# Wkv products from PSUM on VectorE, half-array matmuls in pairs, and a new instruction order in a fused RWKV decoder layer

## The reference

```python
# 1. RWKV layer, on h = layernorm(layernorm(x)); hh is h one token earlier
xk, xv, xr = (h * tm + hh * (1 - tm) for tm in (att_tmk, att_tmv, att_tmr))
k, v, sr = xk @ Wk.T, xv @ Wv.T, sigmoid(xr @ Wr.T)
# wkv, token by token, w = -exp(time_decay), u = time_first:
#   y = (e1*aa + e2*v) / (e1*bb + e2), with qq = max(pp, u + k); then aa, bb, pp move on
x = x + (sr * wkv(w, u, k, v)) @ Wo.T
x = x + sigmoid(xr2 @ Wrec.T) * (square(relu(xk2 @ Wkey.T)) @ Wval.T)
# 2. attention across the 16 heads of one token, causal in the head index, keys and values = ctx
x = x + softmax(mask(q_h . ctx_h / 4)) @ ctx_h
# 3. low-rank FFN of rank 64
x = x + (gelu((x @ U1) @ V1 + b1) @ U2) @ V2 + b2
```

## Time and profile before

| | |
|---|---|
| median of 3 runs | 1357.65 us (1354.46 to 1358.54) |
| the profiled execution's own time | 1354.16 us |
| its span | 1352.4 us |
| instructions | 14723 |
| mean granted TensorE clock | 0.920 |
| DMA | 38.39 MB, 28 GB/s on average |

### The profile page before, as it was taken

The page is one execution under the profiler, slowest core; times in us unless marked ns, Lnnn a source line. Parts: engine busy times, 40 slices in busy tenths (PEclk is TensorE's granted clock), DMA queues, the critical chain, the costliest instruction groups (busy, mean ns, idle before and its releaser), DMA issues.

```text
span 1352.4 us, 14723 instructions
## 1 busy us (share of the span) xinstructions
PE 1090.1 (81%) x3584; PEld 610.2 (45%) x3584; DVE 1076.3 (80%) x2108; ACT 1063.3 (79%) x2134; POOL 982.2 (73%) x847
## 2 busy tenths in 40 slices
PE   0479587979899897979899897979899897959626
PEld 0136354544546363544546363544536363535302
DVE  1454898898989799797989798897989798876681
ACT  8878778888888878888888878888888878566435
POOL 0211896969696988968696978968696978877580
PEclk9889789999999899999999899999999899969667
DMA  5010010001010100101010100101010100110000
GB/s 171 16 38 10 16 32 16 31 17 47 16 47 1 62 0 16 47 16 47 16 47 2 61 0 16 47 16 47 16 47 7 41 1 16 32 32 16 0 16 16
DMA packets 38961, 38.39 MB, mean 28 GB/s; under 512 B 2930, under 2 KB 38644, under 8 KB 38900
## 3 DMA queue, kind: packets, MB, share of 16 engines
q1 hardware_dynamic: 38900, 37.77, 8.7%
HBM read 29.38 MB, written 8.39 MB: 28 GB/s over the span
## 4 chain that ended last, share of the span: by engine, by line
PE 40%; DVE 23%; ACT 18%; POOL 10%; issue 7%; DMA 1%; ACTq 0%; DVEq 0%; POOLq 0%; SPq 0%
PE bank L844 16%; PE bank L920 5%; POOL prod L337 5%; PE bank L926 5%; DVE o_att L1367 5%; PE bank L851 4%; ACT n L470 4%; POOL prod L349 4%; DVE stat L1178 4%; PE bank L912 3%; PE bank L897 2%; PE bank L936 2%; PE bank L930 2%; PE bank L858 1%; DVE num L1289 1%
## 5 line engine op out<-in xcount | busy, mean ns | idle before, releaser
L349 POOL TENSOR_TENSOR prod<-prob,v_dh 128x256 f32<-128x256 f32 (+3 forms) x256 | 404.7, 1617 | 41.4 <-ACT prob L587 23.5
L337 POOL TENSOR_TENSOR prod<-q,kv_ctx 128x256 f32<-128x256 f32 (+5 forms) x448 | 405.6, 944 | 32.9 <-ACT q L470 32.9
L844 PE MATMUL bank<-xk,w_key 128*128 128x512 f32 x512 | 238.4, 614 | 20.2 <-DVE xk L1220 14.2
L1335 DVE TENSOR_REDUCE score<-prod 128x16 f32<-128x256 f32 (+5 forms) x448 | 177.2, 466 | 76.6 <-POOL prod L337 76.6
L897 PE MATMUL bank<-w_val,hidden 128*128 128x256 f32 x1024 | 229.4, 380 | 0.0
L359 POOL TENSOR_TENSOR num<-kT,vT 128x512 f32<-128x512 f32 x32 | 46.6, 1455 | 240.3 <-PE bank L851 181.5
L897 PEld LDWEIGHTS bank<-w_val,hidden 128*128 128x128 f32 x1024 | 193.4, 191 | 31.7 <-issue 7.1
L1367 DVE TENSOR_REDUCE o_att<-prod 128x64 f32<-128x256 f32 (+3 forms) x256 | 189.5, 801 | 10.0 <-POOL prod L349 10.0
L844 PEld LDWEIGHTS bank<-xk,w_key 128*128 128x128 f32 x512 | 98.7, 197 | 142.4 <-issue 117.3
L858 PE MATMUL bank<-ident,n 128*128 128x128 f32 x384 | 63.2, 311 | 123.6 <-ACT n L470 123.6
L858 PEld LDWEIGHTS bank<-ident,n 128*128 128x128 f32 x384 | 51.6, 160 | 150.0 <-issue 147.2
(11 more groups left out here) (104 smaller groups left out, 2159.4 us busy)
## 6 DMA issues: line engine op xcount, KB each, us to landing
x_in<-in_x SPq DMA_DIRECT2D x16, 512.0 KB, 4.9
kv_ctx<-in_ctx SPq DMA_DIRECT2D x16, 512.0 KB, 3.8
n<-in_x SPq DMA_DIRECT2D x16, 512.0 KB, 3.5
out<-y_out SPq DMA_DIRECT2D x16, 512.0 KB, 4.5
w_key<-in_wkey SPq DMA_DIRECT2D x1, 1024.0 KB
w_val<-in_wval SPq DMA_DIRECT2D x1, 1024.0 KB
w_k<-in_wk SPq DMA_DIRECT2D x1, 256.0 KB, 2.7
w_v<-in_wv SPq DMA_DIRECT2D x1, 256.0 KB, 2.9
```

The source lines that it names most:

```text
L337: ins = pool.tensor_tensor(o, a, b, ALU.mult)
L349: ins = pool.tensor_tensor(o, ph[:, HB * n:HB * n + HB, 0:keys].unsqueeze(2).to_broadcast(shape), vh[:, :, 0:keys].unsqueeze(1).to_broadca ...
L844: mm = pe.matmul(to[:, :], w[:, fi, P * f:P * f + P], src[:, fi, :], start=(fi == 0), stop=(fi == CH - 1))
L1335: ins = dve.tensor_reduce(o, src, AX.X, ALU.add)
```

## The change

What is computed stays the same.

1. `kT`, `vT`, `gate_r`, `copy_k` and `copy_v` are gone. `scan_pp`, `rise` read k in `bank[f]`; `gate_of_r` writes its tanh in place into `bank[f]`, and `gate_num` reads it there. v goes to banks 4 and 5 and stays there until `weigh_bonus` has read it. `e2` has a buffer of its own.
2. `weigh_token` and `weigh_bonus` go from POOL to DVE, since v is in PSUM.
3. `project_v1` and `project_u2` are called for pairs of a lower and an upper half; the two one-row matmuls of `open_with_b2` use the array's rows 0 and 64, for which b2 is loaded four times instead of twice.
4. The order of each engine but SP is new. `r` of a half is projected when `rise` has read k from the same bank; `transpose_4` waits for `weigh_bonus` of group i-1 (bank 4 and 5), the second pair of `project_v1` for `gate_num` (banks 0 and 1).

```diff
-    REST_W = 16 * 13
+    REST_W = 16 * 15
+        V_BANK = 4
...
             def gate_of_r(g, f):
                 act.wait_ge(r_mm, upto(g, 2, f + 1))
-                if some(g):
-                    act.wait_ge(gnum_done, upto(g - 1, 2, f + 1))
-                act.activation(gate_r[:, f, :], bank[f][:, :], ACT.Tanh, scale=0.5).then_inc(r_gate, 1)
+                act.activation(bank[f][:, :], bank[f][:, :], ACT.Tanh, scale=0.5).then_inc(r_gate, 1)
...
-                feature_major(bank[2 + f], f, w_v, xv, v_mm)
+                feature_major(bank[V_BANK + f], f, w_v, xv, v_mm)
...
-            def project_u2(g, j):
-                pe.wait_ge(gelu_done, upto(g, 8, j + 1))
-                r = RANK * (j % 2)
-                pe.matmul(bank[4][r:r + RANK, :], w_u2[:, j, :], hidden[:, j, :],
-                          start=(j < 2), stop=(j >= FT - 2)).then_inc(down_mm, 1)
+            def project_u2(g, jj):
+                pe.wait_ge(gelu_done, upto(g, 8, 2 * jj + 2))
+                for j in (2 * jj, 2 * jj + 1):
+                    r = RANK * (j % 2)
+                    pe.matmul(bank[4][r:r + RANK, :], w_u2[:, j, :], hidden[:, j, :],
+                              start=(j < 2), stop=(j >= FT - 2)).then_inc(down_mm, 1)
...
+            def open_with_b2(g):
+                for s in range(2):
+                    r = RANK * s
+                    pe.matmul(bank[s][:, :], ones[r:r + 1, :], b2_row[r:r + 1, :, :].rearrange("p e c -> p (e c)"),
+                              start=True, stop=False)
...
             def scan_pp(g, f):
-                dve.wait_ge(k_out, upto(g, 2, f + 1))
+                dve.wait_ge(k_mm, upto(g, 2, f + 1))
...
+            def weigh_token(g, f):
+                dve.wait_ge(e2_exp, upto(g, 2, f + 1))
+                dve.wait_ge(v_mm, upto(g, 2, f + 1))
+                if f == 0 and some(g):
+                    dve.wait_ge(wo_mm, upto(g - 1, 2))
+                dve.tensor_tensor(num[:, f, :], e2[:, f, :], bank[V_BANK + f][:, :], ALU.mult).then_inc(e2v_done, 1)
+
+            def weigh_bonus(g, f):
+                dve.wait_ge(rr_exp, upto(g, 2, f + 1))
+                dve.wait_ge(aa_done, upto(g, 2, f + 1))
+                dve.tensor_tensor(num[:, f, :], rr[:, f, :], bank[V_BANK + f][:, :], ALU.mult).then_inc(rv_done, 1)
...
```

More of the change, by code:

```diff
@@ L647, in step @@
                     normalise_2(i - 2)
-                act.preload_act_table_set(GELU_SET)
+                if on(4):
+                    variance_ln(4, i - 4)
+                    rstd_of(4, i - 4)
                 if on(1):
-                    gate_of_r(i - 1, 0)
+                    exp_bonus(i - 1, 1)
+                if on(4):
+                    shift_of(4, i - 4)
                 if on(4):
@@ L701, in step @@
                     gelu(i - 4, 3)
-                if on(0):
-                    shift_of(1, i)
+                if on(2):
+                    ffn_now(i - 2, 1)
                 if on(4):
@@ L772, in step @@
                     relu(i - 2, 3)
+                if on(0):
+                    shift_of(1, i)
+                if on(1):
+                    inverse_den(i - 1, 0)
+                if on(2):
+                    square(i - 2, 2)
                 if on(2):
@@ L816, in step @@
                     att_now(i, 0)
-                    att_now(i, 1)
-                if on(1):
-                    inverse_den(i - 1, 0)
-                act.preload_act_table_set(GELU_SET)
                 if on(2):
                     gate_of_rec(i - 2, 1)
-                    values_by_dim(i - 2, p)
                 if on(0):
-                    copy_k(i, 0)
+                    att_now(i, 1)
                 act.preload_act_table_set(EXP_SET)
@@ L1390, in step @@
             def step(i, p, on):
-                if on(2):
-                    stats_2(i - 2, 0)
-                    stats_2(i - 2, 1)
-                    mean_2(i - 2)
                 if on(1):
+                    scan_aa(i - 1, 0)
                     scan_bb(i - 1, 0)
+                    weigh_bonus(i - 1, 0)
+                if on(4):
+                    third_residual(i - 4, p, 1)
+                    stats_4(i - 4, 1)
+                    mean_4(i - 4)
                 if on(3):
@@ L1399, in step @@
                 if on(1):
-                    scan_pp(i - 1, 1)
-                    scan_aa(i - 1, 0)
-                if on(2):
-                    ffn_before_k(i - 2, 0)
+                    weigh_token(i - 1, 1)
+                    scan_aa(i - 1, 1)
+                    weigh_bonus(i - 1, 1)
+                if on(0):
+                    mean_1(i)
+                if on(1):
+                    scan_bb(i - 1, 1)
+                    gate_num(i - 1, 0)
+                    gate_num(i - 1, 1)
                 if on(3):
@@ L1406, in step @@
                 if on(2):
+                    ffn_before_k(i - 2, 0)
+                    ffn_before_k(i - 2, 1)
                     ffn_before_r(i - 2, 0)
@@ L1460, in step @@
                 if on(3):
[L1461 to L1467 removed]
+                    third_residual(i - 3, 1 - p, 0)
                 if on(0):
                     scan_pp(i, 0)
[L1470 to L1471 removed]
+                if on(3):
+                    over_mass(i - 3, 1)
                 if on(0):
```

455 lines of the change are left out of this document (209 added, 246 removed).

## The result

The changed kernel takes 1297.97 us (median of 4 runs, 1295.12 to 1302.84) against 1356.57 of the kernel before on the same chip: ratio 0.9538, 95% interval 0.9500 to 0.9577. The forecast of 1345 and its whole range, 1313 to 1383, lie above it. The profiled execution took 1295.12 us, its span is 1293.2 against 1352.4, and the mean granted clock is 0.923 against 0.920. So 59.2 us of span have to be explained, where I had worked out 10.6 (11 x 0.6 and 4).

What follows compares the result with a forecast made beforehand. No engine fills the span, so the chain of hand-offs, turn A plus B, was taken to decide. 1354.2 - 11 x 0.6 - 4 + 1.7 = 1345.3, said as 1345 us; range 1331 to 1358, whole range 1313 to 1383.

Steps and rivals of the forecast that it cites:

- I cost this at nothing by itself: ACT in the loop: losing four copies and two table loads, 4.9 us a turn, gains nothing except through the order.
- B: Stretch from project_u1 to the next att_before_k: three engines race, DVE last at 38.2 us at the low clock.
- A: Stretch from att_before_k to project_u1: DVE's lead 30.1 plus ACT's 8.0, so 38.1 us, 1.0 longer than before.
- PE's term: PE's part of B: falls by 3.0 us to 37.3 at the low clock, 33.9 at the full one.
- ACT's 2.9: ACT's forming of the mixes between PE's end and att_before_k, 2.9 us, added to PE's 37.3 in B.
- Rival 2: Faster: PE sets B as ACT and DVE keep up; mean turn 73.6 us, 1326 us in all; chance 0.22.
- The clock: Granted clock in the loop: low-clock mix of 0.55 kept, giving -0.8 us a turn, taken as 0.6 for PE's bunched waiting.
- Start and end: Outside the loop: a late store and the slow gate_num of 8.135 us ease; -4 us, between +2 and -12.
- DVE takes the products over: DVE gains POOL's four weighing products, +2.7 us a turn, while operations losing a second SBUF operand save 2.1.
- Rival 3: PE's v1 and u2 pairs: halves overlap already, worth under 1.3 us a turn; inside the forecast, no separate chance.
- Rival 1: Slower: divide_num on DVE meets POOL's value products and lengthens turns; 1366 us, at worst 1389; chance 0.30.
- the prediction's own signs of being wrong: A over 40 or under 36; turn over 77 or under 74; divide_num near 0.7 or 3; att_before_k waiting for ACT or PE.

Runs made afterwards that it cites:

- tables_back: Changed kernel with two more activation table loads a turn on ACT, ahead of ln_den(1) and normalise_1; 1326.48 us, 0.9745 of the kernel before.
- v_in_sbuf: Changed kernel with v copied to SBUF by ACT and the weighings on DVE reading that copy; 1319.59 us, 0.9711 of the kernel before.
- before_pairs: Kernel before with only the v1 and u2 pairs and the two b2 matmuls in rows 0 and 64; 1358.54 us, 1.0014 of the kernel before.
- before_unrolled: Kernel before with its ten hardware-loop turns written out; 1366.92 us, 1.0054 of the kernel before.
- weigh_on_pool: Changed kernel with v copied to SBUF by ACT and the four weighings back on POOL; 1392.23 us, 1.0219 of the kernel before.
- x_again_pool: Changed kernel with add_x_again moved from DVE to POOL; median 1362.61 us against 1354.99 for the kernel before, no ratio given.

## Why the prediction was wrong, point by point

**"I cost this at nothing by itself" (ACT).** This is the step that failed most. The four copies are worth nothing, as said, but putting the two table loads back costs some 30 us (tables_back). I had looked at the loop only, and there at B, where by my sum ACT came at 37.8 and DVE at 38.2: engines that arrive within 1 us of each other have to be shortened together to gain, and here all were. Of the 2.57 us of two loads 1.9 are on the turn, and the start up to the first mark moves by 13.6 to 16.2, where the whole change gained 14.2.

**A, predicted 38.1, is 35.9.** DVE's lead up to mean_4 was worked out as 30.1, with 1.3 of waiting of gate_values for PE; the lead is 713.34 - 684.65 = 28.7, and gate_values (548.53 in the turn above) does not wait. I let project_val's first half come late by rec(1) and left att_before_k where it was; but att_before_k waits for that same rec(1), through att_now, so A starts later with it. ACT's part is 7.2 instead of 8.0. transpose_4(1), which was to be late by 2.2 us, waits 0.71 for weigh_bonus(1); the table load and gate_of_r cover that, but barely, as v_in_sbuf shows.

**B, predicted 35.6 at the full clock with DVE last, is 35.7 with PE and ACT last.** That the length agrees is luck. DVE is ready at 683.4 - 648.9 = 34.5 in a turn with a short add_x_again: the two divide_num cost 2.0 instead of 3.2, and the shifts and add_x_again cost more in the mean (two times 0.5 and 1.1 over the kernel before), partly in places where it waited anyway. In the three turns in which those came together DVE was last, as I had it, with B at 36.9 to 37.0. PE's term was 33.9 with ACT's mixes in it, since 37.3 = 40.3 - 3.0; the sentence that adds "ACT's 2.9" to it counts them twice. Put rec(1)'s 1.73 back, which did not leave the path, and the term is 35.6 against 35.7 measured. That sum has the pairs at 1.3 us; before_pairs shows 1.8 to 2.0 on PE, and in the new order they were not undone by themselves, so how much of the agreement is chance is open.

**Rival 2** named the right mechanism, and its turn of 73.6 is near the measured 73.1, but by two errors of 2 us that cancel: A too long, PE's B too short. The rest of the way from its 1326 to 1298 is the start and the end.

**The clock.** I carried the share of low-clock turns, 0.55, over and even took 0.2 a turn for more of them. Two of ten turns had it, for 4.8 us in all. In its place came the cost of the loop, which no row that I read had set apart: written out, the changed kernel is 11 to 16 us faster (0.9442 against 0.9526, or by the medians), the kernel before is not. All in all the loop's turns exceed the undisturbed one by 1.5 us in the mean (73.1 - 71.6), as those of before did theirs (75.6 - 74.2 = 1.4), so the term that I carried over was right in size and wrong in kind.

**Start and end, predicted -4.** They are -14.2 up to the first mark, -17.3 in the last four turns and -3.2 behind the last. Two table loads a step put back lose 13.6 to 16.2 of the first, as much as was gained there, and 3.6 of the 17.3. (The further loads of b2, which I had at nothing, are two and not four.) Turn by turn the last four gained 4.2, 8.6, 4.3 and 0.2; the gate_num of 8.135 us that the prediction named is not the whole of the 8.6, for before_unrolled has none over 2.64 us and takes 71.4 in that turn, the kernel before 72.9 and the changed one 64.2. The rest stays open.

**DVE takes the products over (+2.7) and loses second SBUF operands (-2.1).** Right, each within 0.2. v_in_sbuf and weigh_on_pool show that this was the change's condition: with v in SBUF 25 us are lost (0.9711 - 0.9526), with the weighings on POOL 94 to 97 (1392.23 against 1297.97 and, on the same chip, 1294.89).

**Rival 3, pairs without effect.** The time of before_pairs (1.0014) looks like it, but the mechanism is refuted: the pairs shorten PE's way from project_u1 to project_v2 by 1.8 to 2.0 us at either clock, and turns without a held gate_num show it. The halves that "overlap already" did not take it away; the gate_num held in five turns did.

**Rival 1.** It was given 0.30. Its sum does not follow as written: 3.2 - 0.8 is 2.4 a turn, which gives 1371 and not 1366. Its mechanism exists, with 8.13 and 9.10 us on divide_num and 8.0 to 8.2 on gate_num in before_pairs, but the changed kernel's divide_num, which does stand in the value products, took 1.0. Why it slips through there and not in x_again_pool was not settled; in both, POOL goes from product to product.

The mis-sized terms in order: start and end by 31 us, A by 2.2 a turn. Three of the prediction's own signs of being wrong came: A is under 36, the mean turn is under 74, and att_before_k waits for ACT.

## What to carry to other kernels

Before an edit is priced at nothing on an engine, ask in each stage, the first and the last steps too, how many us the engine is early, and if that is less than what the edit saves or costs, price it together with the edits on the other engines. An experiment whose time does not change is not yet an edit without effect: read the stretches, for one that shortens PE can send an operation of DVE into a long wait, as before_pairs did. Put one operand of a VectorE operation in PSUM where GpSimd is working beside it: here that is 0.68 us instead of 0.8 to 1.4 in the mean, and no long wait was seen. When the turns of a hardware loop differ in length, look for idle time with the reason "issue" at the jump, and try the loop written out before the order is tuned further.
